# GNN convolution plus soft mixture of experts on one core: the second layer's normalised rows turned by a transposing DMA instead of by TensorE

## The reference

```python
# two graph convolutions: h = x @ W, summed over edges with dinv[src]*dinv[dst], + bias, relu between
x = x + gnn(layernorm(x), W1, b1, W2, b2, edges_with_self_loops)
# soft mixture of experts on the normalised rows
xn     = l2norm(layernorm(x), axis=2)            # 6250 x 768
phin   = scale * l2norm(phi, axis=0)             # 768 x 1024
logits = xn @ phin                               # 6250 x 1024
d_w    = softmax(logits within each expert's 32 slots)
c_w    = softmax(logits over all 1024 slots)
slots  = xn.T @ d_w                              # 768 x 1024, a sum over all rows
eo     = experts(slots)                          # gelu MLP per expert
x      = x + c_w @ eo
```

## Time and profile before

| | |
|---|---|
| median of 3 runs | 3811.48 us (3809.83 to 3813.83) |
| the profiled execution's own time | 3808.86 us |
| its span, first to last instruction | 3807.1 us, 63490 instructions |
| mean granted TensorE clock | 0.966 |
| TensorE (PE) busy | 3299.6 us, 87% |
| weight loads (PEld) | 2087.9 us, 55% |
| VectorE (DVE) | 1811.5 us, 48% |
| ScalarE (ACT) | 1093.5 us, 29% |
| GpSimd (POOL) | 1727.0 us, 45% |
| gathers' queue (q0) and plain transfers' queue (q1), share of the 16 DMA engines | 50.1% and 24.7% |

### The profile page before, as it was taken

How to read it: one execution, slowest core, us unless ns; L and a number is a source line. 1 busy time by engine, 2 the same in 40 slices (tenths; PEclk the granted TensorE clock), 3 DMA queues, 4 the chain that set the end, 5 groups by cost and what they waited for, 6 DMA issues and landing times. The chain is left out here.

```text
span 3807.1 us, 63490 instructions
## 1 busy us (share of the span) xinstructions
PE 3299.6 (87%) x20875; PEld 2087.9 (55%) x20875; DVE 1811.5 (48%) x2830; ACT 1093.5 (29%) x1313; POOL 1727.0 (45%) x1692
## 2 busy tenths in 40 slices
PE   7204999999999999969999999999999954479998
PEld 6102666666666666645556556556556521146665
DVE  8685233333333333227777777777777740021111
ACT  3652222222222222214344344344344310011110
POOL 0103766666666666547666656666666400000000
PEclk9997999999999999989999999999999987789999
DMA  8264988888888888759888888888888649934443
GB/s 341 95 264 148 319 287 288 287 284 291 288 282 291 289 280 292 256 186 349 293 302 298 298 294 299 296 295 298 307 288 300 233 149 351 321 130 151 151 152 126
DMA packets 265456, 994.14 MB, mean 261 GB/s; under 512 B 38306, under 2 KB 67260, under 8 KB 265200
## 3 DMA queue, kind: packets, MB, share of 16 engines
q0 software_dynamic: 133728, 656.12, 50.1%
q1 hardware_dynamic: 131472, 334.56, 24.7%
HBM read 867.64 MB, written 122.89 MB: 260 GB/s over the span
## 5 line engine op out<-in xcount | busy, mean ns | idle before, releaser
L1139 POOL DMA_INDIRECT m_ring<-table,idx x833 | 877.8, 1054 | 539.8 <-PE m_part L1300 308.6
L872 POOL DMA_INDIRECT a_ring<-table,idx x833 | 833.7, 1001 | 480.7 <-PE a_part L976 300.5
L1300 PE MATMUL m_part<-m_ring,m_pick 128*128 128x512 f16 (+1 forms) x3332 | 598.3, 329 | 11.4 <-DMA m_ring<-table,idx 10.2
L976 PE MATMUL a_part<-a_ring,a_pick 128*128 128x512 f16 (+1 forms) x3332 | 580.4, 327 | 10.2 <-DMA a_ring<-table,idx 9.3
L1300 PEld LDWEIGHTS m_part<-m_ring,m_pick 128*128 128x128 f16 x3332 | 418.9, 142 | 155.2 <-issue 23.3
L976 PEld LDWEIGHTS a_part<-a_ring,a_pick 128*128 128x128 f16 x3332 | 413.6, 142 | 137.8 <-issue 18.9
L1315 PE MATMUL m_ps_s<-m_dw,m_xn 128*128 128x512 f16 x1764 | 428.8, 380 | 12.1 <-DVE slots L1198 12.1
L1626 PE MATMUL c_po<-c_eh,c_cT 128*128 128x512 f16 (+1 forms) x1568 | 328.8, 327 | 12.3 <-DVE c_cT L1595 12.3
L1328 PE MATMUL m_ps_l<-phi_h,m_xT 128*128 128x512 f16 x1176 | 309.8, 379 | 0.3 <-issue 0.2
L1315 PEld LDWEIGHTS m_ps_s<-m_dw,m_xn 128*128 128x128 f16 x1764 | 171.5, 98 | 183.7 <-issue 19.4
L1198 DVE TENSOR_TENSOR slots<-slots,m_ps_s 128x512 f32<-128x512 f32 x288 | 196.5, 683 | 150.5 <-PE m_ps_s L1315 150.5
(11 more groups left out here) (354 smaller groups left out, 4204.4 us busy)
## 6 DMA issues: line engine op xcount, KB each, us to landing
e_w1s<-in_L_ffn_w_dram SPq DMA_DIRECT2D x32, 1152.0 KB, 14.8
e_w2s<-in_L_ffn_w_dram SPq DMA_DIRECT2D x32, 1152.0 KB, 13.6
cw_dram<-m_cst SPq DMA_DIRECT2D x49, 512.0 KB
c_cw<-cw_dram SPq DMA_DIRECT2D x49, 512.0 KB, 4.7
x_pad<-xs SPq DMA_DIRECT2D x7, 2688.0 KB, 24.0
table<-stage SPq DMA_DIRECT2D x49, 384.0 KB, 2.3
a_own<-table SPq DMA_DIRECT2D x49, 384.0 KB, 4.3
table<-a_stage SPq DMA_DIRECT2D x49, 384.0 KB, 2.8
```

The costliest lines, as they stand in the source:

```text
L872: pool.indirect_dma_start(out=ring[:, t, :], out_offset=None, in_=table, in_offset=bass.IndirectOffsetOnAxis(ap=idx[:, k:k + 1], axis=0)). ...
L976: mm = nc.tensor.matmul(part[:, bass.ds(to + a, z - a)], pick[:, i % 2, :, t], ring[:, t, half * D + a:half * D + z], start=False, stop=(t ...
L1139: pool.indirect_dma_start(out=ring[:, t, :], out_offset=None, in_=table, in_offset=bass.IndirectOffsetOnAxis(ap=idx[:, n:n + 1], axis=0)). ...
L1300: mm = nc.tensor.matmul(part[:, bass.ds(off + at, e - f)], pick[:, i % 2, :, t], ring[:, n % RING, half * D + f:half * D + e], start=False ...
```

## The change

The tile `ps_t`, the twelve turns of a bundle on TensorE and the two copies are gone. In their place SP issues one transposing DMA for each bundle, from the 128 x 1536 numbers of `xn` in SBUF to `xT` in SBUF, now 12 blocks of 128 x 128. It is issued in SP's round `i` for bundle `j = i - 2`, behind the load of `xb` and ahead of the store of the combining weights, once `xn_hi` and `xn_lo` of the bundle are there and the logits of the bundle before it have been made (since they read the same `xT`). TensorE's logits wait for the transfer's semaphore `xn_turned` instead of for the copies. No other order is changed.

```diff
--- before.py
+++ after.py
@@ -1044,7 +1044,7 @@
         tmp = sb("tmp", [P, D], F32)
         xb = sb("xb", [P, 2, D], F32)
         xn = sb("xn", [P, XN, 2, D], F16)
-        xT = sb("xT", [P, 2, D], F16)
+        xT = sb("xT", [P, 2 * DC, P], F16)
         lg = sb("lg", [P, K], F32)
         dwf = sb("dwf", [P, K], F32)
         dw = sb("dw", [P, DW, 2, K], F16)
@@ -1061,7 +1061,6 @@
         Z = sb("Z", [P, 1], F32)
         rZ = sb("rZ", [P, 1], F32)
         part = ctx.enter_context(nc.psum_tensor("m_part", [P, 3 * 512], F32))
-        ps_t = ctx.enter_context(nc.psum_tensor("m_ps_t", [P, 1024], F16))
         ps_l = ctx.enter_context(nc.psum_tensor("m_ps_l", [P, K], F32))
         ps_s = ctx.enter_context(nc.psum_tensor("m_ps_s", [P, 2, 512], F32))
         gathered = [sem(f"gathered{t}") for t in range(RING)]
@@ -1069,10 +1068,10 @@
         x_in = [sem(f"x_in{s}") for s in range(2)]
         x2_out = [sem(f"x2_out{s}") for s in range(2)]
         cw_out = sem("cw_out")
-        (cleared, picked, consumed, evicted, zeroed, scaled_u, x2_r, stats, var_r, rooted, coef, xn_hi, xn_f, xn_lo, hi_turned, lo_turned,
-         xt_hi, xt_lo, logits, lg_r, maxed, shifted, expd, cexp, zs, dwf_r, dw_hi, dw_lo, rz_r, cw_hi, cw_lo, unit_r, added) = (sem(n) for n in (
+        (cleared, picked, consumed, evicted, zeroed, scaled_u, x2_r, stats, var_r, rooted, coef, xn_hi, xn_f, xn_lo, xn_turned,
+         logits, lg_r, maxed, shifted, expd, cexp, zs, dwf_r, dw_hi, dw_lo, rz_r, cw_hi, cw_lo, unit_r, added) = (sem(n) for n in (
              "cleared", "picked", "consumed", "evicted", "zeroed", "scaled_u", "x2_r", "stats", "var_r", "rooted", "coef", "xn_hi", "xn_f",
-             "xn_lo", "hi_turned", "lo_turned", "xt_hi", "xt_lo", "logits", "lg_r", "maxed", "shifted", "expd", "cexp", "zs", "dwf_r", "dw_hi",
+             "xn_lo", "xn_turned", "logits", "lg_r", "maxed", "shifted", "expd", "cexp", "zs", "dwf_r", "dw_hi",
              "dw_lo", "rz_r", "cw_hi", "cw_lo", "unit_r", "added"))
         dve = sem("dve")
         OWN = ((0, 0, 512), (1024, 512, D))
@@ -1121,6 +1120,11 @@
                         wait(sp, xn_f, i - 1)
                         wait(sp, x2_out[i % 2], 16 * (i // 2))
                         sp.dma_start(xb[:, i % 2, :], x_pad[bass.ds(b * P, P), :]).then_inc(x_in[i % 2], 16)
+                    if 0 <= j < NBR:
+                        sp.wait_ge(xn_hi, j + 1)
+                        sp.wait_ge(xn_lo, j + 1)
+                        wait(sp, logits, j)
+                        sp.dma_start(xT[:, :, :], xn[:, j % XN, :, :].rearrange("p h d -> p (h d)"), transpose=True).then_inc(xn_turned, 16)
                     k = i - 3
                     if 0 <= k < NBR:
                         b3 = own_block(sp, tab, k)
@@ -1164,10 +1168,6 @@
                         nc.scalar.activation(dwf[:, :], dwf[:, :], ACT.Exp).then_inc(expd, 1)
                         act.wait_ge(maxed, k + 1)
                         nc.scalar.activation(lg[:, :], lg[:, :], ACT.Exp, bias=nM[:, 0:1], accum_out=Z[:, 0:1]).then_inc(cexp, 1)
-                    if 0 <= j < NBR:
-                        act.wait_ge(hi_turned, j + 1)
-                        wait(act, logits, j)
-                        nc.scalar.activation(xT[:, 0, :], ps_t[:, 0:D], ACT.Copy).then_inc(xt_hi, 1)
                     if 0 <= k < NBR:
                         act.wait_ge(dwf_r, k + 1)
                         wait(act, unit_r, dw_free(k))
@@ -1266,10 +1266,6 @@
                         link(v.reciprocal(Z[:, :], Z[:, :]))
                         v.tensor_scalar(rZ[:, :], Z[:, :], PS, None, ALU.mult).then_inc(rz_r, 1)
                     add(i, 2)
-                    if 0 <= j < NBR:
-                        v.wait_ge(lo_turned, j + 1)
-                        wait(v, logits, j)
-                        v.tensor_copy(xT[:, 1, :], ps_t[:, 0:D]).then_inc(xt_lo, 1)
                     if 0 <= k < NBR:
                         v.wait_ge(dw_hi, k + 1)
                         v.tensor_tensor(dw[:, k % DW, 1, :], dwf[:, :], dw[:, k % DW, 0, :], ALU.subtract).then_inc(dw_lo, 1)
@@ -1319,13 +1315,12 @@
                     if i < NBR:
                         w = pe.value_load(tab[0:1, 4 * i:4 * i + 1], min_val=0, max_val=2 ** CT)
                     if 0 <= k < NBR:
-                        pe.wait_ge(xt_hi, k + 1)
-                        pe.wait_ge(xt_lo, k + 1)
+                        pe.wait_ge(xn_turned, 16 * (k + 1))
                         wait(pe, lg_r, k)
                         for c in range(DC):
                             for half, ph in ((0, phi_h), (0, phi_l), (1, phi_h)):
                                 for a in (0, 512):
-                                    mm = nc.tensor.matmul(ps_l[:, a:a + 512], xT[:, half, c * P:(c + 1) * P], ph[:, c, a:a + 512],
+                                    mm = nc.tensor.matmul(ps_l[:, a:a + 512], xT[:, half * DC + c, :], ph[:, c, a:a + 512],
                                                           start=(c == 0 and half == 0 and ph is phi_h), stop=(c == DC - 1 and half == 1))
                         mm.then_inc(logits, 1)
                     if i < NBR:
@@ -1344,20 +1339,8 @@
                     unit(1)
                     steps(5, 8)
                     unit(2)
-                    if 0 <= j < NBR:
-                        pe.wait_ge(xn_hi, j + 1)
-                        wait(pe, xt_lo, j)
-                        for c in range(DC):
-                            mm = nc.tensor.transpose(ps_t[:, c * P:(c + 1) * P], xn[:, j % XN, 0, c * P:(c + 1) * P], ident16[:, :])
-                        mm.then_inc(hi_turned, 1)
                     steps(8, 11)
                     unit(3)
-                    if 0 <= j < NBR:
-                        pe.wait_ge(xn_lo, j + 1)
-                        pe.wait_ge(xt_hi, j + 1)
-                        for c in range(DC):
-                            mm = nc.tensor.transpose(ps_t[:, c * P:(c + 1) * P], xn[:, j % XN, 1, c * P:(c + 1) * P], ident16[:, :])
-                        mm.then_inc(lo_turned, 1)
                     steps(11, 14)
                     unit(4)
                     steps(14, CT)
```

## The result

| | before | changed |
|---|---|---|
| median | 3810.65 us (3809.31 to 3813.83, 4 runs) | 3989.05 us (3975.28 to 3994.40, 4 runs) |
| ratio to the kernel before | 1 | 1.0461, 95% interval 1.0432 to 1.0490 |
| span of the profiled execution | 3807.1 us | 3991.2 us |
| mean granted TensorE clock | 0.966 | 0.945 |

Times are medians of repeated executions; one execution of an experiment's kernel (the half change, third chip), at a granted clock of 0.617, took 6137 us and is left out.

The account below looks back on a forecast made before the run. TensorE was taken to bound the second layer, DMA engines next. From 3808.86 us, - 33 (turns) - 2 (wait for ScalarE's copy) + 4 (first rounds) gave 3778, a median of about 3781 us; own range 3774 to 3797, 8-in-10 range up to 4000.

Parts of the forecast that it names:

- TensorE is the bound, and its 0.67 us a bundle come off in full: Second layer: twelve turns a bundle leave fully busy TensorE, 33 us over 49 bundles, period 28.35 to 27.68 us.
- The copies cost nothing: The two copies, 0.79 us on ScalarE and 0.56 us on VectorE, lie beside TensorE's full queue; nothing counted for them.
- SP's queue: The new DMA's issue on SP may last up to 12 us before anything behind it is late; nothing counted.
- The DMA engines' time: The transfer's own work a bundle: 1536 pieces of 256 bytes, 1.7 us on each engine, ends 1.0 and 11.5 us.
- the X of my formula: Transfer's time on all 16 engines; the period is the larger of 27.68 and 23.7 + X us.
- The room, 4.0 us, and the break-even at 4.65 us: DMA engines have 4.0 us free a bundle; above that the gain shrinks, above 4.65 us it becomes a loss.
- The landing: Transfer ahead of the logits lands in about 8 us of the 13.6 us available once the turns are gone.
- The clock: TensorE's granted clock falling below 1.00 in the new gaps was named as a sign of a wrong forecast.
- The first rounds, 4 us: First four rounds, engines already full: transfers add some 7 us, of which perhaps 4 reach TensorE past the ring.
- The rivals: Slower cases: full DMA engines, 0.23; blocks one behind another, 4580 us, 0.10; number by number, over 8000 us, 0.07.
- the signs of full engines: DMA share 0.98, waits at TensorE's sums for gathered rows, gathers landing well over 5.8 us; rival's chance 0.23.
- the signs of a late landing: Wait ahead of the logits, period 14.1 us plus the landing; decides past 13.6 us; blocks-in-series chance 0.10.

Follow-up runs that it names:

- the half change: Kernel before with only the rows' high half turned by a six-block transfer, low half by TensorE: ratio 0.9944 on the second chip, 1.0009 (3812.61 us) on the third.
- the plain copy: Changed kernel with each bundle's turning transfer made a plain copy of the same bytes, place and waits, blocks not turned: 3781.26 us, ratio 0.9922.
- the short gathers: Changed kernel with all 17 gathers of a bundle, each row 1536 bytes instead of 3072: 3780.94 us, ratio 0.9922.
- the two runs in which nobody waits for a late landing: Kernel before plus a turning transfer into an unread tile, 3923.78 us; changed kernel with two turned tiles and logits one bundle late, 3936.97 us.
- one round more to land: Changed kernel with two turned tiles, logits made from the rows turned for the bundle before: 3936.97 us, ratio 1.0346.

## Why the prediction was wrong

- **TensorE is the bound, and its 0.67 us a bundle come off in full**: right, by the plain copy (period 27.6 us, 3781.26 us) and by the short gathers (3780.94 us).
- **The copies cost nothing**: consistent with the same two runs, not tested apart.
- **SP's queue**: the issue was taken as short. It measures 2.6 us in the median and up to 8.9 us, inside the 12 us that I had allowed. In the two runs in which nobody waits for a late landing it is about 9 us in the median, and up to 14.3 us.
- **The DMA engines' time, "I take 1.7 us"**: this is the step that failed. For a plain transfer of the same packets it is exact (1.7 us), and for the turning transfer without company nearly so (2.1 us). Beside the gathers it is 5.4 us of packet time in the change, and the gathers, for which I had no term, have 2.4 us more. I had priced the transfer by its own packets, as though a packet's price did not depend on what else is on the engine. All the rows that I used for prices were of copies. Since packet times overlap, the X of my formula is better read from the period of the two runs in which only the load acts: 29.6 and 29.8 us are 23.7 + X for X of about 6 us.
- **The room, 4.0 us, and the break-even at 4.65 us**: with X of about 6 us both are passed, and the formula then gives a loss of 60 to 70 us; those two runs lost 93 and 85 us in their profiled executions. As a sharp edge neither is confirmed: 1.05 us of plain copy gives the whole gain, but 1.7 us in small packets gives none, by its late landing, and the half change's 3.5 us give none either.
- **The landing, "5.9 + 1.7 and somewhat more"**: the second thing to fail, by the same step: 13.7 us in the median and up to 27.6 us, instead of 8. Even plain packets of 256 bytes land in 11.1 us, three more than I gave them. In the steady part 88.0 of TensorE's 93.8 idle us are this wait.
- **The clock**: I had named its fall as a sign of being wrong and put nothing in the sum for it. It fell to 0.94, which costs 0.9 us a bundle, some 45 us of the layer. It follows the waits: it is 1.00 in the steady part of every run in which TensorE is full.
- **The first rounds, 4 us**: before 1800 us TensorE waits 22.8 us for gathered rows in the change, against 3.7 us before.
- **The rivals**: neither came as I had drawn it. Of the signs of full engines the share (0.99) and the landing of the gathers (11.1 us) are there, but in the steady part not the waits at the sums. Of the signs of a late landing the wait ahead of the logits is there, but the period of 32.4 us is longer than 14.1 plus the landing's 14.5. The two are tied: the landing is late because of the gathers beside it (4.7 us without them), and one round more to land moves the wait to the sums and gives back only about 45 us. So load, landing and clock share the loss where I had given two of them a case each and the third none; how it splits between them is known only roughly. The blocks do not go one behind another: twelve land in 3.6 us when alone.

The Trainium skill (DMA: Bandwidth & Descriptors, section "Rules for kernel authors") says of a turning transfer that next to ordinary DMAs it "needs nothing". That stands in a row on corrupted results, so it speaks of correctness. The 261 GB/s of its section "Latency and other measured facts" are more than what the lone transfer reached here, 393 KB in 2.1 us, or 187 GB/s. Neither says what the company of gathers does to it; the traces here put that at two and a half times its packet time alone, or more.

That a turning packet waits in the engine or at the crossbar until other packets have passed is my reading of the durations, which follow the gathers' packet length: four rows of the table with long packets, one with short ones. Where the packet stands while it waits no record shows.

## What to carry to other kernels

The transposing DMA had two prices here: a small one when the DMA engines had nothing else, and another, two and a half times the first or more, with late gathers on top, when long gathers ran beside it. Before trading a few hundred nanoseconds of TensorE for it, look at the DMA share in that stretch: at 0.85 the trade lost 178 us, with the gathers' packets shortened and their bytes halved it won 30. Look also where the waits are in the steady part alone: the waits of the whole layer, 127 us at the logits and 45 us at the sums, mix the first rounds with it. And add packet times up with care: they came to 1.08 of the time. A second transfer that nobody waits for, put beside the old way, prices the load in one run; a plain copy in its place shows what the rest of the change is worth.

## What was not expected of the hardware

- A 256-byte packet of a turning transfer mostly takes 18 ns, and else mostly once or twice the length of a packet of the gathers beside it (some 240 and 500 ns with packets of 6144 bytes, 120 to 200 and 280 to 400 ns with packets of 3072 and 4608 bytes).
- The gathers suffer too, but not always in packet time: they had 19.5 us a bundle before and 21.9 us in the change, with the same bytes, yet 19.2 and 19.7 us in the two runs in which nobody waits for a late landing. What grew in all three is their landing, from 5.8 us to 11.1, 14.4 and 13.9 us.
- The mean busy share of the DMA engines can pass 1 (1.08 and 1.07 in those two runs).
- A copy in 256-byte packets beside gathers lands in 11.1 us and costs 24 us of 3781, though it loads the engines with only 0.7 us a bundle more than one in large packets (1.7 against 1.05 us).
- The issue of a transposing DMA holds SP for 1.45 us at least and 8.9 us at most in the change (14.3 us in the run with one round more), against 0.34 us for a plain one.
